# A four-layer stack of attention and feed-forward: in the last head attention, one values product for four query heads, with high and low shares stacked in the rows; the text stage's end in another order

## The reference

```python
# third feed-forward (text stage)
xn = rms_norm(x); scale = 127.0 / clip(max(abs(xn)), EPS)
xq = clip(round(xn * scale), -128, 127) / scale
x + gelu(einsum('bsd,od->bso', xq, wq) + b)

# fourth attention: H = 32 query heads, KVH = 8 key/value heads, HD = 128
q = rmsnorm(hidden @ Wq.T, q_norm_w); k = rmsnorm(ctx @ Wk.T, k_norm_w); v = ctx @ Wv.T
k, v = repeat(k, 4 heads), repeat(v, 4 heads)
probs = softmax(q @ k.T / sqrt(HD) + mask)
out = (probs @ v).reshape(rows, H * HD) @ Wo.T
```

## Time and profile before

| | us |
|---|---|
| median of 3 runs (lowest, highest) | 3316.93 (3313.36, 3325.38) |
| the profiled execution | 3323.23 |
| its span, first to last instruction | 3321.4 |
| TensorE busy | 3180.1 (96%) |
| VectorE busy | 1708.0 (51%) |
| ScalarE busy | 1476.6 (44%) |
| GpSimd busy | 1126.5 (34%) |
| a weight load of 512 KB, issue to landing (median) | 3.4 |

### The profile page before, as it was taken

How to read it: one execution, slowest core, us unless ns; L and a number is a source line. 1 busy time by engine, 2 the same in 40 slices (tenths; PEclk the granted TensorE clock), 3 DMA queues, 4 the chain that set the end, 5 groups by cost and what they waited for, 6 DMA issues and landing times. The chain is left out here.

```text
span 3321.4 us, 55551 instructions
## 1 busy us (share of the span) xinstructions
PE 3180.1 (96%) x21708; PEld 2528.0 (76%) x21708; DVE 1708.0 (51%) x3700; ACT 1476.6 (44%) x3294; POOL 1126.5 (34%) x689
## 2 busy tenths in 40 slices
PE   8998999999999999999999979999999999999997
PEld 5666568888888888888754447888788878888885
DVE  5887543334333433333443666555655655556554
ACT  5776234444444444444322444444444444444443
POOL 6775322232332233222120113333333333344322
PEclk9999999999999999999999989999999999999999
DMA  3000121121122112211012012222111212222201
GB/s 107 2 2 5 40 92 61 64 83 58 64 64 75 66 58 65 64 64 64 14 60 111 13 40 83 69 70 82 64 64 65 82 58 70 70 64 70 73 30 58
DMA packets 56566, 199.93 MB, mean 60 GB/s; under 512 B 8976, under 2 KB 9744, under 8 KB 53008
## 3 DMA queue, kind: packets, MB, share of 16 engines
q1 hardware_dynamic: 56336, 196.76, 17.6%
HBM read 192.54 MB, written 4.19 MB: 59 GB/s over the span
## 5 line engine op out<-in xcount | busy, mean ns | idle before, releaser
L1757 POOL TENSOR_TENSOR h_wol<-h_ro,h_woh 128x1024 fp32r<-128x1024 f32 x128 | 314.4, 2456 | 611.1 <-ACT h_woh L1808 611.1
L1753 POOL TENSOR_TENSOR h_wql<-h_rq,h_wqh 128x1024 fp32r<-128x1024 f32 x128 | 309.0, 2414 | 501.9 <-ACT h_wqh L1803 501.9
L2254 DVE COPY h_tf<-ps 128x512 f32<-128x512 f32 (+1 forms) x256 | 142.6, 557 | 607.2 <-PE ps L2035 607.1
L2258 DVE TENSOR_TENSOR h_ol<-ps,h_oh 128x512 fp32r<-128x512 f32 x256 | 176.8, 691 | 524.1 <-ACT h_oh L1861 524.1
L141 PE MATMUL ps<-h_woh,h_oh 128*128 128x512 f32 x1024 | 427.8, 418 | 5.9 <-DVE h_ol L2258 5.8
L141 PE MATMUL ps<-h_Xh,h_wqh 128*128 128x512 f32 x1024 | 415.1, 405 | 4.1 <-ACT h_sq L1847 1.9
L143 PE MATMUL ps<-h_woh,h_ol 128*128 128x512 f32 x1024 | 405.6, 396 | 0.0
L142 PE MATMUL ps<-h_wol,h_oh 128*128 128x512 f32 x1024 | 404.8, 395 | 0.0
L143 PE MATMUL ps<-h_Xh,h_wql 128*128 128x512 f32 x1024 | 401.7, 392 | 0.0
L142 PE MATMUL ps<-h_Xl,h_wqh 128*128 128x512 f32 x1024 | 400.4, 391 | 0.0
L1911 ACT ACTIVATE h_ex<-ps,h_mx 128x128 f32<-128x128 f32 x512 | 181.3, 366 | 270.8 <-DVE h_mx L2294 270.7
(11 more groups left out here) (298 smaller groups left out, 6316.5 us busy)
## 6 DMA issues: line engine op xcount, KB each, us to landing
h_rq<-in_L_Wq SPq DMA_DIRECT2D x128, 512.0 KB, 3.4
h_ro<-in_L_Wo SPq DMA_DIRECT2D x128, 512.0 KB, 3.4
h_rk<-in_L_Wkv SPq DMA_DIRECT2D x47, 512.0 KB, 3.4
h_craw<-in_ctxT SPq DMA_DIRECT2D x7, 1024.0 KB, 5.7
cnat<-in_ctx SPq DMA_DIRECT2D x4, 1024.0 KB, 8.9
t_craw<-in_ctxT SPq DMA_DIRECT2D x4, 1024.0 KB, 8.7
t_cn<-in_ctx SPq DMA_DIRECT2D x4, 1024.0 KB, 5.3
out_rows<-x SPq DMA_DIRECT2D x16, 256.0 KB, 2.5
```

The lines of the kernel that those rows point to most:

```text
L1753: nc.gpsimd.tensor_tensor(wql[:, par], rq[:, par], f(wqh[:, par]), ALU.subtract).then_inc(m["p_wq"], 1)
L1757: nc.gpsimd.tensor_tensor(wol[:, par], ro[:, par], f(woh[:, par]), ALU.subtract).then_inc(m["p_wo"], 1)
L2254: nc.vector.tensor_copy(tf[:], ps[:, TBK, 0:PT]).then_inc(m["v_t"], 1)
L2258: nc.vector.tensor_tensor(by_head(ol), ps[:, AB, :].rearrange("p (b h t) -> p b h t", h=2, t=S), f(by_head(oh)), ALU.subtract).then_inc(m[ ...
```

## The change

The last head attention gets a function of its own, `phase_heads_last`, a copy of `phase_heads` for this case with these differences:

- The shares of one sequence lie in `tp` as high shares in one half of the rows and low shares in the other. ScalarE writes the high ones (`shares_high`, two casts of 64 rows), VectorE the low ones into the other half (`shares_out`, two subtractions of 64 rows). The values lie in `vh` twice, in both halves, and their low share in `vl` in the half of the high shares, with zeros in the other.
- `values_of` multiplies four query heads at a time: for one half of the sequences and two sequences of it, four fp32r matmuls over 256 columns. It runs four steps behind, the output product six steps behind.
- The values are copied by ScalarE (`values_high`, two copies of 64 rows) and VectorE (`values_in`, two copies and two subtractions of 64 rows) in t=0 of the next iteration.
- In t=3 the output product is split, one half ahead of the wait for the turned keys' copy and one behind `turn_shares`. The output weights are cast in t=1 and t=2 of the next iteration. The raw weights `rq` and `ro` have one buffer each. The loop over i=3..5 is written out. `keys_norm` works in place, the exponentials too.

In the text stage the last group's statistics come before the linear results of the group before, the additions of that group after `quantize`, and its `gelus` after `ternary_rows`; `quantize` takes the largest value tile by tile and scales and adds in one operation.

```diff
@@ text stage, ScalarE @@
-                            nc.scalar.preload_act_table_set(LN_EXP)
+                            if g != G - 2:
+                                nc.scalar.preload_act_table_set(LN_EXP)
...
+                        ternary_rows(G - 1)
                         gelus(G - 2)
-                        ternary_rows(G - 1)
@@ text stage, VectorE @@
-                            dve.wait_ge(q_xn, NT * g + NT)
-                            own(nc.vector.tensor_reduce(qs[:, 2], rn[:], AX_X, ALU.max, apply_absolute_value=True))
+                            for i in tiles(g):
+                                dve.wait_ge(q_xn, i + 1)
+                                last = nc.vector.tensor_reduce(qs[:, 2, i % NT:i % NT + 1], rn[:, i % NT], AX_X, ALU.max,
+                                                               apply_absolute_value=True)
+                            own(last)
...
-                                last = nc.vector.tensor_scalar(rn[:, j], rn[:, j], qs[:, 3, j:j + 1], -128.0, ALU.mult, ALU.max)
+                                last = nc.vector.tensor_scalar(rn[:, j], rn[:, j], qs[:, 3, j:j + 1], MAGIC, ALU.mult, ALU.add)
                             own(last)
-                            own(nc.vector.tensor_scalar(rn[:], rn[:], MAGIC, None, ALU.add))
...
                             add_output(g)
+                            if g + 1 == G:
+                                ternary_stats(g)
                             if g:
                                 linear_out(g - 1)
-                        ternary_stats(G - 1)
-                        ternary_add(G - 2)
                         ternary_scale(G - 1)
                         quantize(G - 1)
+                        ternary_add(G - 2)
@@ the new function, against phase_heads @@
+                    if t == 3 and not (g == G - 1 and type(i) is int and i + AHEAD >= NKV):
+                        kv(it + AHEAD, wrap(i + AHEAD, NKV))
+                    if t in (1, 2) and it:
+                        k = 2 * (it - 1) + t - 1
+                        o(k, k % NP)
...
+                        def shares_high(n):
+                            act.wait_ge(m["s_t"], n)
+                            wait(act, m["s_av"], 2 * half_index(n) - 4)
+                            for b in range(2):
+                                r = slice(64 * b, 64 * b + 64)
+                                nc.scalar.copy(shares_at(n)[r, b::2, :], turned_shares(r)).then_inc(m["a_th"], 1)
...
+                        def values_of(U):
+                            it, half = U // 4, U % 4 // 2
+                            pe.wait_ge(m["v_t"], 4 * it + 3 + half)
+                            wait(pe, m["v_o"], U)
...
+                            for b in range(2):
+                                b4 = 2 * (U % 2) + b
+                                for z in (vh, vl):
+                                    last = nc.tensor.matmul(ps[:, AB, 2 * P * b:2 * P * (b + 1)], z[:, HB * half + b4],
+                                                            tp[:, (2 * it + half) % 3, b4].rearrange("p z q -> p (z q)"),
+                                                            start=z is vh, stop=z is vl)
+                            last.then_inc(m["s_av"], 1)
...
+                                    if t == NS - 1:
+                                        wait(pe, m["v_t"], n - 1)
+                                        turn_keys(it + 1)
+                                        if early:
+                                            output(n - 6, (0,))
+                                        pe.wait_ge(m["a_k"], it + 2)
...
+                                    turn_shares()
+                                if early:
+                                    output(n - 6, (1,))
+                                elif n >= 6:
+                                    output(n - 6)
...
+                        def shares_out(n):
+                            dve.wait_ge(m["s_t"], n)
+                            wait(dve, m["s_av"], 2 * half_index(n) - 4)
+                            for b in range(2):
+                                r = slice(64 * b, 64 * b + 64)
+                                dve.wait_ge(m["a_th"], 2 * n - 1 + b)
+                                last = nc.vector.tensor_tensor(shares_at(n)[64 - 64 * b:128 - 64 * b, b::2, :], turned_shares(r),
+                                                               f(shares_at(n)[r, b::2, :]), ALU.subtract)
+                            last.then_inc(m["v_t"], 1)
```

577 lines of the change are left out of this document (576 added, 1 removed).

## The result

The changed kernel takes 3515.93 us (median, 3514.78 to 3518.66) against 3316.66 us for the kernel before on the same chip: 1.0598 times as long, 95% interval 1.0577 to 1.0619. The profiled execution has a span of 3516.9 us, 195.5 us more than before's 3321.4. The prediction was 3475 us with a range from 3270 to 3505: right in direction and in its main mechanism, the lost start, but 41 us too low.

What follows compares the result with a forecast made beforehand. TensorE was taken to bound the kernel before, with VectorE's lost race making steps late after the change. Profiled execution 3323.2+161-5+1 = 3480 us, standing 6.3 above the median, so 3475; range 3270 to 3505.

Steps and rivals of the forecast that it cites:

- the lost start: Steady steps: GpSimd's weight subtraction starts before VectorE's product of the shares, which then takes 2.65 us instead of 0.42.
- TensorE's part: Values product: 0.98 us becomes 0.48, saving 0.50 a step, 2.0 an iteration; bound by TensorE alone, 35.8 us an iteration.
- The race: VectorE's product of the shares loses to GpSimd's subtraction by about 0.07 us, costing 2.2 each; lost in all steps, chance 0.42.
- the working: Start times followed through VectorE, GpSimd, ScalarE and TensorE in steps t=0 to t=3, with the race lost.
- The sum for an iteration: Steady iteration: 35.8+4.0+1.9+1.7 = 43.4 us against 38.2, +161 us over some 31 iterations.
- the list of signs: What would show it: among others, TensorE waiting some 4 us in t=3 for the keys' copy and a 43 us iteration.
- Ends of the stage: Last head attention's start and end: work moves from first steps to the end; 0 us, bounds -10 and +10.
- Text: Text stage's end: largest value in parts, scaling and adding in one operation, earlier statistics; -5 us (-3 to -6).
- Clock: Rival: waits lower the granted clock in the steady stage; at a mean of 0.97, 30 us more, 3505 us; no chance given.
- VectorE keeps its lead: Rival: the product of the shares still starts before GpSimd; 38.2 us an iteration, about 3313 us (3300 to 3333); chance 0.16.
- The step on queues: Sync queue's weight loads with single buffers: 0 us in steady state, 1 us once at the stage's start.
- TensorE's saving shows: Rival: keys' scaling clears GpSimd; 37.3 us an iteration and 3283 us, or 3235 with no wait; chance 0.30.

Runs made afterwards that it cites:

- e7: e1 with key weights' load early, queries' and keys' copies ahead of t=3's exponentials, and keys' sum, scaling and root early in t=2: 3293.1 us.
- e8: e7 with the third row turning moved to t=3 of the fourth head and the last two output weights split into the query weights' buffers: 3274.7 us.
- e1: Changed kernel with VectorE's sum, reciprocal and product of the shares ahead of its two low-share subtractions: 3365.2 us.
- e2: Changed kernel with GpSimd's weight subtraction in each step waiting for VectorE's product of the shares: 3386.1 us.
- e9: e8 with VectorE's low shares put back ahead of its product of the shares in t=0, t=1 and t=3: 3367.0 us.
- e4: Kernel before with only the text stage's end reordered as in the change: 3314.9 us, ratio 0.9990.
- e5: e1 with the sync queue issuing the next key and value weights' load in t=0 instead of t=3: 3343.4 us.
- e6: e1 with ScalarE's copies of the queries and turned keys in t=3 ahead of that step's exponentials: 3364.8 us.

## Why the prediction was right, and where it was off

**TensorE's part.** Right in kind, too large. From the product's first matmul (2544.41) to the scores (2545.06) are 0.65 us, where 0.98 were the earlier trace rows: the last three matmuls start 0.12 us apart as forecast, but the second starts 0.20 behind the first and the scores 0.21 behind the fourth, and I had compared the sum of pitches, 0.48, with a stretch from start to start. The saving is 0.33 us a step, 1.3 an iteration. Bound alone by TensorE I had 35.8 us; e7 and e8 show 36.8, 1.4 below before and not 2.4.

**The race.** Right in place, cause and size: GpSimd leads by 0.14 us (0.07 forecast), the product takes 2.5 us (2.65), and 123 of 128 steps lose. From VectorE's first low share to the product are 1.55 us (2564.72 to 2566.27), 1.56 by the working; GpSimd starts 1.41 behind that low share, 1.49 by the working. e1, e2 and e9 show it by intervention. The forecast gave this case a chance of 0.42, and 0.07 us was hardly more than the 0.05 to which its terms were good: which side of zero it fell on was not safe.

**The sum for an iteration.** By the working's parts the steps take 9.3, 12.0, 10.3 and 11.8 us; they are 9.4, 12.1, 10.4 and 11.9. That closeness is in part luck: in the iteration at 3258.20 TensorE's own part is 36.9 us and not 35.8, and its waits are 6.9 us and not 7.6, two errors that mostly cancel. The waits stand where the working had them, 2.37 us at the square (2.3 by the working) and 1.34 at the keys' copy, 3.7 for 4.0; only the list of signs, which put all 4 us at the copy, had the place wrong. The mean gain in length over 31 iterations is 5.6 us and not 5.2: +173.7 for +161, 13 us of the miss.

**The term that failed: "Ends of the stage", 0 with bounds of -10 and +10.** This is the step that failed, and the larger part of the miss. It measured +26.9. The two halves of that estimate were not of one kind. Outputs moved out of the first steps free nothing, because those are bound by the chain, as I had written: the first iteration takes 36.1 us, before 35.5. The same outputs at the end are all on the path: six outputs of 2.8 us and four values products stand behind the last shares, where there were two and one. The rows of the changed kernel, then of the kernel before, from the last turned shares (L2822, L2035) to the feed-forward part's first turned rows (L1037):

```profile
3416.73 0.44 PE L2822 MATMUL ps<-ident,h_pr 128*128 128x128 f32 x2 [3.23 <-DVE h_pr L3052]
...
3423.25 0.44 PE L2822 MATMUL ps<-ident,h_pr 128*128 128x128 f32 x2 [1.27 <-DVE h_pr L3052]
...
3442.17 0.76 PE L141 MATMUL ps<-h_woh,h_oh 128*128 128x512 f32 x1 [4.86 <-POOL h_wol L2596]
...
3457.47 1.06 PE L1037 MATMUL ps<-ident,xn 128*128 128x128 f32 x8 [1.37 <-PEq L2544]
```
```profile
3249.15 0.44 PE L2035 MATMUL ps<-ident,h_pr 128*128 128x128 f32 x2
...
3261.99 1.06 PE L1037 MATMUL ps<-ident,xn 128*128 128x128 f32 x8 [1.37 <-PEq L1705]
```

Between them lie 34.2 us where there were 12.8, so 21.4 of the 26.9: four outputs and three values products more (some 12.7 us), 5.7 us more of waiting, most of it the 4.86 for the last weights, and some 3 us because two of the outputs run in part at the lower clock (4.45 and 4.27 us for 2.8). The other 5.5 us lie ahead of the last turned shares and are the race again: TensorE waits there for the late product. The feed-forward part behind is as long as before, 59.4 us. In e7, with no start lost, the stretch from the last iteration's start to the feed-forward part is 62.2 us, in e8 58.2; it was 67.8 in the changed kernel and 40.9 before.

So the failed step is a term of the sum that took the work moved to the end for hidden, where it is on the path. In the profiled execution the miss is 38.5 us (3518.7 for 3480.2), and the iterations' 12.7 with the ends' 26.9 make it up to 1 us. The rest stands on the way to the median: the profiled execution is 2.7 us above its median and not 6.3 (and 3480 less 6.3 is 3474, not 3475).

**Text.** -5 forecast. e4 has 3.4 (0 to 7), the traces' means 5.7 at the scores' first start.

**Clock.** That rival's condition came true, 0.96 over the stage against 0.99, but not its price in steady iterations: 0.96 and 1.00 give the same 43.8 us, because the slower matmuls fill time that TensorE would wait for the keys' copy. The price shows where nothing else is waited for: some 3 us at the stage's end. Where groups begin it is open.

**The rivals' prices.** "VectorE keeps its lead" gave 38.2 us an iteration; e5 has 38.3 in steady iterations and e1 38.9. But its total, 3313, was too low by the same ends and by the late load: e1 is 3365, in its trace 22.8 us longer than before behind the last iteration's start and 28.6 in the iterations, 24.8 of which e5's earlier load takes away. The step on queues, "0 in steady state", holds for the changed kernel, where no wait for the key weights shows, and fails once VectorE is on time: 24.6 us in e1, 63.4 in e6. I had looked at the output weights' load, not at the key weights' load that stands behind it. "TensorE's saving shows" was right about its condition, that the keys' scaling clear GpSimd: e7 does that and reaches 36.8 us and 3293.

**Open.** Why iteration lengths after a group's start stay up for some iterations in the changed kernel was not tried. The clock can have a part in it: the first iteration of the second group takes 50.3 us at a granted clock of 0.93, that of the third 47.5 at 0.96 (before, 44.9 and 46.4), and no run separates the two. Nor was a drain with fewer outputs behind the last shares.

## What to carry to other kernels

Where a VectorE operation with two inputs in SBUF and a GpSimd operation are both released by the same engine's work, write down the lead of one over the other: 0.14 us the wrong way cost 1.1 to 1.2 us a step here, and putting the VectorE operation one place earlier in its own queue gave 151 of 200 us back. When one wait goes and the time stays, look for the same wait under another name before dropping the fix: e6 alone was worth nothing, and its trace has the same wait at a load two places down the sync queue; together with that load and the keys' order moved, 72 us came back. And price a longer pipeline's fill and drain apart: the drain is on the path even where the fill saves nothing.

## What the runs showed of the hardware

- The blocked product ends 0.29 us behind the end of GpSimd's subtraction (2568.79 against 2568.50), less than the 0.42 us that it takes alone. So it isn't slowed down beside GpSimd but held nearly whole; where the other 0.13 us of it are spent the rows don't show.
- GpSimd is not slowed by the VectorE operation that it blocks: 2.37 to 2.40 us with and without one waiting. A second subtraction right behind, at 2568.47, takes 2.53, with the held product running until 2568.79. Where VectorE gets in between two subtractions it is GpSimd that waits: the second took 2.85 us in e1 (2872.12), while the keys' scaling was running to 2872.71.
- On ScalarE a pair of half-row casts lasts 0.74 to 0.76 us, 0.37 each, with no overlap, as on VectorE (0.86).
- TensorE's matmuls over 512 columns start 0.23 us apart at a granted clock of 1.00 and 0.43 apart at 0.50 (2571.40 to 2574.78, behind 2.37 us of waiting). 3.38 us at that level cost nothing where the chain through VectorE set the pace, and 1.6 us of a step in e6.
